# Splitting the gate weights in their natural layout and transposing them by DMA on the sync queue

## The reference

```python
gate0 = jnp.einsum('bld,ehd->bleh', x, gating_w[:, 0])
gate1 = jnp.einsum('bld,ehd->bleh', x, gating_w[:, 1])
act = jax.nn.gelu(gate0) * gate1
out = jnp.einsum('bleh,ehd,ble->bld', act, linear_w, combine)
```

## Time and profile before

| | |
|---|---|
| median of 3 runs | 1682.9 us (1676.08 to 1683.25) |
| the profiled execution, its own time | 1678.45 us |
| its span, first to last instruction | 1676.7 us |
| mean granted TensorE clock | 0.964 of full speed |
| busy: PE / DVE / ACT / POOL | 89% / 71% / 55% / 35% of the span |
| one full step (issue of line 552 to the next) | 74.4 us |

### The profile page before, as it was taken

One profiled execution on the slowest core, in us unless ns is written; L12 is line 12 of the kernel. 1 busy time (PEld: TensorE's weight loads), 2 busy tenths in 40 slices (PEclk: granted clock), 3 DMA queues, 4 the chain that ended last, 5 costly groups with the idle time before them and its releaser, 6 DMA issues.

```text
span 1676.7 us, 35791 instructions
## 1 busy us (share of the span) xinstructions
PE 1493.0 (89%) x12510; PEld 1085.1 (65%) x12510; DVE 1195.3 (71%) x3240; ACT 922.1 (55%) x2526; POOL 589.2 (35%) x775
## 2 busy tenths in 40 slices
PE   3799999999999999999999999999765499999994
PEld 2567676767767676767767676776553266666662
DVE  5478788888878888887978888887763344445442
ACT  4276666767666676767666676766641133333331
POOL 3011333242323333232333324232333356555552
PEclk9899999999999999999999999999877699999997
DMA  7201021020202012020201102010400363333334
GB/s 249 70 1 64 14 64 58 20 77 2 77 8 71 26 52 71 7 76 1 77 14 64 65 14 77 2 58 8 164 32 0 105 173 61 60 59 58 58 61 123
DMA packets 77836, 98.12 MB, mean 59 GB/s; under 512 B 20400, under 2 KB 61376, under 8 KB 77600
## 3 DMA queue, kind: packets, MB, share of 16 engines
q1 hardware_dynamic: 51152, 77.01, 14.1%
q0 software_dynamic: 15680, 18.69, 6.8%
q10 hardware_dynamic: 10832, 0.13, 0.3%
HBM read 64.89 MB, written 35.10 MB: 60 GB/s over the span
## 4 chain that ended last, share of the span: by engine, by line
PE 62%; DVE 18%; ACT 7%; POOL 5%; issue 3%; SPq 2%; DMA 2%; ACTq 0%; POOLq 0%; DVEq 0%
PE S L1282 11%; PE W L949 9%; PE W L951 9%; PE W L950 9%; PE T L954 7%; PE O L1302 6%; PE O L1053 4%; POOL routing_table L693 4%; PE S L1027 3%; DVE mx L1462 3%; ACT prob L785 2%; DVE pTl L1474 2%; PE W L954 2%; PE W L1158 2%; PE W L1138 2%
## 5 line engine op out<-in xcount | busy, mean ns | idle before, releaser
L785 ACT ACTIVATE prob<-S,nm 128x256 f32<-128x256 f32 x512 | 235.5, 474 | 80.8 <-DVE nm L1465 54.1
L778 ACT ACTIVATE pTh<-T 128x512 f16<-128x512 f32 x256 | 139.3, 597 | 137.1 <-PE T L954 136.9
L634 POOL TENSOR_SCALAR ve_ln<-mv_ln 128x2 f32<-128x2 f32 x64 | 14.6, 229 | 472.8 <-DVE mv_ln L1436 471.9
L1462 DVE TENSOR_REDUCE mx<-S 128x2 f32<-128x512 f32 x256 | 163.3, 679 | 21.2 <-PE S L1027 20.7
L1282 PE MATMUL S<-GL,xgh 128*128 x568 | 169.8, 381 | 2.7 <-DVE xgl L1756 2.7
L1474 DVE SCALAR_TENSOR_TENSOR pTl<-T,pTh 128x512 f16<-128x512 f32 x256 | 164.1, 682 | 6.4 <-ACT pTh L778 6.4
L716 POOL DMA_INDIRECT acc_rows<-ysb,tab x71 | 112.3, 1582 | 134.2 <-DMA acc_rows<-ysb,tab 90.3
L794 ACT ACTIVATE prob<-prob,rden 128x256 f32<-128x256 f32 x256 | 116.5, 504 | 56.4 <-DVE p0n L1483 55.7
L954 PE MATMUL T<-ident,prob 128*128 128x128 f32 x1024 | 141.5, 282 | 1.8 <-DVE prob L1487 1.7
L949 PE MATMUL W<-cTh,Wkh 128*128 128x256 f16 x512 | 140.6, 275 | 0.0
L950 PE MATMUL W<-cTl,Wkh 128*128 128x256 f16 x512 | 140.5, 274 | 0.0
(11 more groups left out here) (293 smaller groups left out, 4325.1 us busy)
## 6 DMA issues: line engine op xcount, KB each, us to landing
cx<-in_ctx_dram SPq DMA_DIRECT2D x16, 512.0 KB
gst<-in_L_ffn_gating_w_dram SPq DMA_DIRECT2D x16, 512.0 KB
gating_split<-gsp SPq DMA_DIRECT2D x16, 512.0 KB
GL<-gating_split SPq DMA_DIRECT2D x8, 1024.0 KB
stg<-in_L_xattn_Wkv_dram SPq DMA_DIRECT2D x8, 512.0 KB, 13.5
xl<-in_x_dram SPq DMA_DIRECT2D x16, 256.0 KB
lst<-in_L_ffn_linear_w_dram SPq DMA_DIRECT2D x16, 256.0 KB
xres<-in_x_dram SPq DMA_DIRECT2D x16, 256.0 KB
```

The costliest lines, as they stand in the source:

```text
L778: A(flat(pTh[:, h, :, :]), T[h][:, :], ACT.Copy).then_inc(s_pTh[h], 1)
L785: ins = A(prob[:, h, t, :], S[h][:, t * NTOK:(t + 1) * NTOK], ACT.Exp, bias=nm[:, h, t:t + 1], scale=SM, accum_out=rs[:, h, t:t + 1])
L1462: ins = V.tensor_reduce(mx[:, h, :], S[h][:, :].rearrange("p (t k) -> p t k", t=TT), AX.X, ALU.max)
```

## The change

`gating_units` and both "gT" units are removed; "rank" becomes the 30th unit in place of the 32nd and gets bank 2 in place of bank 1. ACT makes the high part straight from `gst` in SBUF, still untransposed, to a new buffer `gsn`, at j = 6 behind `attn_high(2)`. DVE makes the low part from `gst` and `gsn`, at its old place. SP waits for that, issues two transposing DMAs (256 KB each, SBUF to SBUF, `gsn` to `gsp`), waits until both have landed, and then stores `gsp` as before. To make room, `x4` shares the buffer of `xh`, and `x4T` that of `xn`; for this, DVE's wait for the store of `x4` moves from ln4 (j = 7) to ln2 (j = 2).

```diff
--- before.py
+++ after.py
@@ -51,7 +51,7 @@
          ("k", True, PRE), ("v", True, PRE),
          ("xhT", True, POST), ("v", True, PRE), ("win", False, POST),
          ("v", True, PRE), ("v", True, PRE), ("x4T", False, POST), ("logits", False, POST),
-         ("gT", True, ATTN), ("gT", True, ATTN), ("rank", False, POST)]
+         ("rank", False, POST)]
 NWORK = 3
 LOOP_START, LOOP_STEPS = 2, NB - 4
 
@@ -295,8 +295,8 @@
         arg = sb("arg", [P, 2, NTOK])
         dec = sb("dec", [P, 2, NTOK])
         x3 = sb("x3", [P, TT, D])
-        x4 = sb("x4", [P, TT, D])
-        x4T = sb("x4T", [P, KD, NTOK])
+        x4 = xh
+        x4T = xn
         st = {n: sb("st_" + n, [P, TT, 6]) for n in ("ln1", "lno", "ln2", "ln3", "ln4")}
         mv = {n: sb("mv_" + n, [P, TT, 2]) for n in st}
         rstd = {n: sb("rstd_" + n, [P, TT]) for n in st}
@@ -322,6 +322,7 @@
         rec = sb("rec", [P, TT * TOPK, 2], I32)
         gst = sb("gst", [P, 4, D])
         lst = sb("lst", [P, 2, D])
+        gsn = sb("gsn", [P, 2, KD, 4, P], FP16)
         gsp = sb("gsp", [P, 2, KD, HID], FP16)
         lsp = sb("lsp", [P, 2, 2, D], FP16)
 
@@ -371,6 +372,7 @@
         s_c = [sem("ctx_in0"), sem("ctx_in1")]
         s_xr = sem("xres_in")
         s_gw = sem("gating_in")
+        s_gh, s_gl, s_gT = sem("gating_high"), sem("gating_low"), sem("gating_transposed")
         s_lw = sem("linear_in")
         full = [sem(f"work_full{k}") for k in range(NWORK)]
         half = [sem(f"work_high{k}") for k in range(NWORK)]
@@ -547,8 +549,11 @@
                 if POST in parts:
                     rows_out(i, post, work)
                 if ATTN in parts:
-                    for k, nfull, _ in work.at["gT"]:
-                        wait_apart(sp, free[k], nfull)
+                    wait_apart(sp, s_gl, i.n + 1)
+                    for c in range(2):
+                        sp.dma_start_transpose(gsp[:, c, :, :].rearrange("p m (c r) -> p (m c) r", r=P),
+                                               gsn[:, c, :, :, :].rearrange("p m c d -> p (m c d)")).then_inc(s_gT, 16)
+                    wait_apart(sp, s_gT, 32 * (i.n + 1))
                     sp.dma_start(pick(gsplit_d, i.n), gsp[:, :, :, :].rearrange("p a b c -> p (a b c)"))\
                       .then_inc(s_go, 16)
                     wait_apart(sp, s_lsp, i.n + 1)
@@ -888,6 +893,11 @@
                             v_high(1)
                         if attn:
                             attn_high(2)
+                            act.wait_ge(s_gw, 16 * (i.n + 1))
+                            at_least(act, s_gT, 32 * i.n)
+                            for m in range(KD):
+                                ins = A(gsn[:, 0, m, :, :], gst[:, :, m * P:(m + 1) * P], ACT.Copy, scale=WS)
+                            ins.then_inc(s_gh, 1)
                     if j == 7:
                         if pre:
                             v_high(2)
@@ -899,9 +909,6 @@
                             whole("x4T", flat(x4T[:, :, :]))
                         if attn:
                             prob_high(j)
-                            at_least(act, s_go, 16 * i.n)
-                            for m in range(2):
-                                one("gT", m, gsp[:, 0, m, :], WS)
                             attn_high(3)
                         if post_:
                             act.wait_ge(s_dl, post.n + 1)
@@ -1158,14 +1165,6 @@
                             ins = M(o[:, c], dec[:, k, tok], u[post.par][:, k, :], start=False, stop=(k == 1))
                     ins.then_inc(s, 1)
 
-                def gating_units():
-                    pe.wait_ge(s_gw, 16 * (i.n + 1))
-                    for m in range(KD):
-                        o, s = bank("gT", m)
-                        for c in range(4):
-                            ins = tr(o[:, c * P:(c + 1) * P], gst[:, c, m * P:(m + 1) * P])
-                        ins.then_inc(s, 1)
-
                 def logits_unit():
                     evicted("x4T")
                     o, s = bank("logits")
@@ -1256,7 +1255,6 @@
                         if post_:
                             logits_unit()
                         if attn:
-                            gating_units()
                             values(j)
                         if post_:
                             rank_unit()
@@ -1622,6 +1620,7 @@
                         if pre:
                             low("xT", 0, flat(xTl[:, :, :]), flat(xTh[:, :, :]))
                     if j == 2 and post_:
+                        dve.wait_ge(s_x4o, 16 * (post.n + 1))
                         normed("ln2", post, xh, tiles(x1), rstd["ln2"]).then_inc(s_nrm["ln2"], 1)
                     if j == 5 and post_:
                         ffn_residual()
@@ -1691,7 +1690,6 @@
                             attn_low(2)
                     if j == 7:
                         if post_:
-                            dve.wait_ge(s_x4o, 16 * (post.n + 1))
                             normed("ln4", post, x4, tiles(x3), rstd["ln4"]).then_inc(s_nrm["ln4"], 1)
                         if pre:
                             dve.wait_ge(s_rstd["ctx"], nxt.n + 1)
@@ -1707,8 +1705,11 @@
                         if post_:
                             select()
                         if attn:
+                            dve.wait_ge(s_gh, i.n + 1)
                             for m in range(KD):
-                                low("gT", m, gsp[:, 1, m, :], gsp[:, 0, m, :], WS)
+                                ins = V.scalar_tensor_tensor(gsn[:, 1, m, :, :], gst[:, :, m * P:(m + 1) * P], WS,
+                                                             gsn[:, 0, m, :, :], ALU.mult, ALU.subtract)
+                            ins.then_inc(s_gl, 1)
                         if post_:
                             take_ranks()
                         if attn:
```

## The result

| | before | after |
|---|---|---|
| median of 7 runs each | 1680.32 us (1676.08 to 1683.25) | 1692.44 us (1687.65 to 1699.17) |
| ratio | | 1.0074, 95% interval 1.0051 to 1.0097 |
| the profiled execution, its own time | 1678.45 us | 1699.17 us |
| mean granted TensorE clock | 0.964 | 0.947 |
| full step without a wait at `add_residual` | 74.37 us | 74.31 us |

The change costs 12 us (0.74%). The new time lies inside the range of 1672 to 1726 us, but 8 us above the predicted 1684 and outside that case's own range (1676 to 1690). It is also past the 0.5% that the prediction named as about what a measurement can tell from no change. The profiled execution after is the slowest of the seven, so its excess of 20.7 us over the one before is larger than that of the medians.

The account below looks back on a forecast made before the run. TensorE bounds most of a step, but VectorE's chain, then GpSimd's scatters, its end. Full steps 0, step 0 +0.5, step 15 -0.4 and +1.0: +1.1 us, 1684.0 on the median; range 1672 to 1726.

Parts of the forecast that it names:

- X: SyncE's wait at each step's end for the transposing DMAs to land, delaying stores and loads: 2.6 to 24 us, taken as 8.
- the scatters' term of the sum: GpSimd's four scatters at a step's end still land in time despite the delayed burst of stores and loads: 0 us.
- rival B: Slower, 22%: at step ends the delayed burst falls on the scatters, at most 43 us (1726), about 1704 for half.
- deadline of +15.6: Scatter landings cost nothing until 15.6 us after the `gsp` store's original issue point, as `add_residual` stands at +16.6.
- With X = 8 the last scatter lands by about +10: At a step's end the last scatter is out at +7.5, lands by about +10; burst begins at about +9; cost 0.
- Rival C: Slower, 9%: past X = 14 scatter packets stand behind the transposing DMAs; at X = 20, 62 us more, 1746.
- TensorE: 0: Removing TensorE's `gst` transposes, 1.0 us a step, gains 0, because they lie inside its wait for VectorE.
- rival D: Faster, 10%: TensorE's time at the step ends counts after all, 16 us less, 1667.
- The clock part of rival E: TensorE's clock falls because it now idles twice at the step's end; no separate size, within a rival of 4%.
- ScalarE: hidden, 1.1 us: Two new SBUF operations at j = 6, 1.1 us, hidden in the 2.63 us idle before `pTh`; step 0 taken +0.5.
- VectorE: 0: The two `gsp` low parts reading SBUF, 0.69 us against 682 ns, plus moved `x4` wait and shared buffers: 0.
- Step 15 and 16: At the last step end: -0.4 us from TensorE's removed transposes, +1.0 from transposes and store beside the last scatters.

Follow-up runs that it names:

- e10: The changed kernel, transposing transfers issued but not waited for, SyncE storing untransposed `gsn` at once: 1695.98 us, ratio 1.0091.
- e7: The changed kernel with two plain copies of the same size in place of the transposing transfers, still waited for: 1696.27 us, ratio 1.0102.
- e5: The changed kernel with the pair of transposing transfers made twice, each pair waited for: 1680.06 us, ratio 1.0011.
- e11: The kernel before with SyncE held until VectorE's first maxima of the next step, store 3.84 us late, no added transfer: 1689.22 us, ratio 1.0052.
- e3: The kernel before with SyncE held until ScalarE's first exponentials of the next step, store 5.8 us late, no added transfer: 1683.02 us, ratio 1.0020.
- e6: The changed kernel with transposing transfers and `gsp` store moved behind the next step's loads: 1680.97 us, ratio 1.0014.
- e12: The kernel before with SyncE held until VectorE's `xn` of the next step, store 10.3 us late, no added transfer: 1679.51 us, ratio 0.9998.
- e1: The changed kernel with GpSimd's wait for the four scatters moved from before `rstd["lno"]` to late in the step: 1676.01 us, ratio 0.9983.
- e2: The kernel before with GpSimd's wait for the four scatters moved from before `rstd["lno"]` to late in the step: 1676.03 us, ratio 0.9983.
- e4: The changed kernel without the transposing transfers and their wait, the store reading untransposed `gsn`: 1676.45 us, ratio 0.9988.

## Why the prediction was right and wrong

**The step that failed** is the size of X, taken at 8 us as the middle of 2.6 and 24, and with it the scatters' term of the sum, taken at 0. X measures 4.5 to 6.7 us, inside the window of 3.5 to 7.5 that rival B named; the burst fell on the scatters and the term was +12. Of a quantity known only within a factor of nine, with a bad window inside that range, the middle was used as if it were a measurement. That 1692 us still lies inside the stated range is not to the credit of this sum: the range reached up to 1726 because rival B's bound was put into it. The two bounds held, and the lower one, from plain transfers, was the nearer: X is 1.7 to 2.6 times the 2.6 us, and 3.6 to 5.3 times under the 24.

The figure of the Trainium skill for a DMA transpose of 128x128, 1309 ns ("VectorE: DVE Perf Modes", The three transpose paths), added up over sixteen blocks, gave an estimated 21 us. The sixteen blocks took 4.5 to 6.7, so the measurement decides against adding blocks up. The 261 GB/s of the Trainium skill ("DMA: Bandwidth & Descriptors", Latency and other measured facts) gave an estimated 2 us plus fixed costs. That was the nearer, if too fast: after moves 179 and 211 GB/s in the two full microseconds of a pair (215 to 217), and of 4.47 us in step 7, 2.61 are issue.

**Rival B** was right in mechanism, deadline and sign, and its window held the X that was measured. The window's lower end was not right: with the store at 2.7 (e10) and mostly 3.0 us (e7), under its 3.5, the cost is the highest of all. The deadline of +15.6 holds closely: in e5, e11 and after, seams with `ve_lno` at up to +15.5 have no wait, and one at +15.95 waits 0.37 us. Its price, 43 at most and about 22 for half, was too high for the change: only 4 of the 14 seams land beyond +15.6 (at +19.3, +19.6, +15.95, +16.6). The nine slow seams of before do not move by X each. One part was missing from it: the clock. In after, e3 and e11, waits of 1.87 us or more go with steps longer by the wait and another 1.6 to 2.9 us (e11: 2.04 us of wait, 78.27 in place of 74.37), and TensorE works at 0.50 for a while behind them. Two steps of e6 point to the clock: with a wait of 1.80 us and a clock of 0.50 in 312 to 314 the step is 1.9 us longer than the wait explains (78.04), with a wait of 1.95 us and the clock at 1.00 all through it is 0.1 us longer (76.36).

**"With X = 8 the last scatter lands by about +10"** is half right. In e12 the burst begins at +10.3 and costs nothing, but GpSimd sees landings as late as +15.0, not +10, although the packets are out by +8.5; what saves them is the deadline. Rival C is refuted up to X = 15.4: there `ve_lno` comes at +15.3 in e5, and at +15.0 in the same seam of e12, with no transposing transfer at all. X = 20 was not tried.

**TensorE: 0, against rival D's 16 us.** Right. With the landing wait out of the way the change is worth 0.0 us (e1 against e2). Taking transposes and transfers both away (e4) brings 2 us (interval 0.2 to 3.7), which is not more than moving the wait alone does in e2. The full step fell by 0.06 us, from 74.37 to 74.31. The chain's 62% on TensorE said nothing about this place; the two rows at the place did.

**The clock part of rival E** was dismissed on the ground that TensorE already idled 3.7 us in each step at clock 1.00. That reasoning failed. Every kernel that takes the transposes off TensorE shows its clock fall at 7 to 9 of 14 step ends, every one that keeps them (before, e2, e3, e11, e12) at none. Windows of 1 us in e1, at the end of step 2; in front of them TensorE idles for 0.84 us ahead of `values(7)`, where before it had the transposes, and for 0.86 us ahead of the ranks (0.92 in e2, which keeps the transposes, and there the clock stays at 1.00):

```profile
284.00:285.00 1.00, 0.30 (x6) 0.03 (x1) 0.90 (x8) 0.67 (x2) 0.16 (x1) 1.00 0.03 8
285.00:286.00 1.00, 0.84 (x13) 0.67 (x15) 1.00 (x3) 0.02 (x1) 0.00 (x0) 0.72 0.00 0
286.00:287.00 1.00, 1.00 (x10) 0.45 (x7) 0.97 (x4) 0.00 (x0) 0.00 (x0) 0.50 0.00 0
287.00:288.00 1.00, 1.00 (x7) 1.00 (x6) 0.93 (x9) 0.37 (x1) 0.00 (x0) 0.50 0.49 98
288.00:289.00 1.00, 1.00 (x7) 0.93 (x6) 0.93 (x7) 0.00 (x0) 0.16 (x1) 0.57 0.97 179
```

The price is small, since VectorE's chain sets the end there: a step of 75.0 us now and then (one in e1; four of 75.0 to 76.4 in e4 beside others of 74.3). The traces tie these steps to the clock: over all runs, of the full steps without a wait at `add_residual`, the eighteen of 74.9 us or more are just those at whose start the clock stays near 0.50 for six of the windows of 1 us, up to +5, in place of two or three. What decides between the two lengths is open, and no run put idle transposes back to test it.

**ScalarE: hidden, 1.1 us.** Right: its pair takes 1.14 us (step 7 of after), and the gap before `pTh` shrinks from 2.63 to 1.61. **VectorE: 0.** Right: 684 ns with the weights in SBUF against 682 with them in PSUM, forecast 0.69 us. The moved wait for `x4` and the shared buffers cost nothing in e1. **SyncE's loads** are late by up to 7.4 us (e1), 15.4 us (e5), and nothing waits for them. **Step 15 and 16:** -0.4 was forecast for step 15, and it takes 72.13 us in e1 against 72.41 in e2. +1.0 was forecast for the last scatter; `add_residual` of step 16 waits 3.6 us more in after. Nothing of that shows in e1, where the wait stands later.

Rows of after for the two operations (groups by line and shape):

```profile
L1710 DVE SCALAR_TENSOR_TENSOR gsn<-gst,gsn 128x512 f16<-128x512 f32 x32 | 20.6, 684 | 0.0
...
L899 ACT ACTIVATE gsn<-gst 128x512 f16<-128x512 f32 x32 | 18.3, 624 | 0.0
```

**Open:** what makes a landing late. It is late with the packets out: in e12 the last scatter's packets pass by 294.0 and GpSimd sees the landing at 300.47; SyncE's burst, begun in between, moves only 30 GB/s from 298.5 to 300.5 and 279 GB/s right behind. It is also late with the packets held back, as in the seam of 292.92, where the burst stands still too. So the overlap makes the lateness larger, but something in these seams is slow without it. Open is also why most of them lie in the first steps, in before too (`ve_lno` at up to +15.5, against +11.3 to +13.1 from step 8 on), and why that of step 12 joins them in e7, e10 and e11 (+17.6 to +18.7).

The Trainium skill says that an engine serves its queues in turn, packet by packet ("DMA: Bandwidth & Descriptors", Queues, rings and completion order). By that rule the 32 small packets of the last scatter need not wait for the end of the burst. In the seam of 292.92 they do pass before it ends, but 8 us late; the rule does not say why.

## What to carry to other kernels

Moving work from a busy engine to a transfer gained nothing here, since the engine was waiting at that place anyway; look at the row in front of and behind the work, not at the engine's share. When a step delays a queue, ask what the burst behind it will then lie on: small transfers with a waiting engine behind them, here four scatters whose latest landings come 0.1 to 0.3 us before they are due, are the ones that pay. The cost need not grow with the delay (8.7 us at 3.8 us of delay, 3.4 at 5.8, 0 at 10.3, with nothing else changed). And look first whether that wait can be moved: here it brought both kernels to 1676.0 us, 0.17% below before, which no version of the change improved.

## What the runs showed of the hardware that was not expected

- Two transposing transfers of 256 KB each, SBUF to SBUF, take 2.6 us to issue and 4.5 to 6.7 us to land (of 16 in after, eight near 4.5, the others at 5.3 or more); two plain copies of the same bytes 3.0 to 5.7 us.
- A burst put on top of small indirect transfers delays them, and is itself slowed: `ve_lno`, at +11.3 to +15.5 in before, comes at up to +19.6, and the burst moves 3 to 28 GB/s for 6 us where that of before moves 302.
- The landing of an indirect transfer was seen up to 6 us and more behind its last packet (e12: 294.0 and 300.47).
- Twice the transfers was faster than once (1680.06 against 1692.44 us).
- TensorE's granted clock fell to 0.50 after gaps of 0.84 and 0.86 us (e1), for 3 to 7 us, at 7 to 9 of 14 step ends, where with the transposes in place it stayed at 1.00 at all 14; and after each of the eight waits of 3.0 to 4.1 us at `pTl`, in after, e3, e7, e10 and e11.
